# Query and key projected feature-major, split in the read stage and reloaded as stacked operands

## What is computed

```python
x = res.reshape(b, l, H, C)                                  # H 512, C 4
y = jnp.einsum('blhc,hoc->bloh', x, W)                       # then normalised over h
q = jnp.einsum('bli,oi->blo', q, qkv_w[0]).reshape(b, l, NH, HD)   # NH 16, HD 32; k, v alike
q = rope(q, pos); k = rope(k, pos)     # x1*cos - x2*sin, x2*cos + x1*sin
scores = jnp.einsum('bqhd,bkhd->bhqk', q, k) / np.sqrt(HD)   # causal mask
p = jax.nn.softmax(scores, axis=-1)
o = jnp.einsum('bhqk,bkhd->bqhd', p, v)
```

## Time and profile before

| | us |
|---|---|
| median of 3 runs | 2198.38 |
| lowest and highest | 2197.77, 2211.18 |
| the profiled execution: span | 2198.0 |
| setup and read stage | 0 to 342.4 |
| attention | 342.4 to 846.4 |
| block stage | 846.4 to 2198.0 |

### The profile page before, as it was taken

The page is one execution under the profiler, slowest core; times in us unless marked ns, Lnnn a source line. Parts: engine busy times, 40 slices in busy tenths (PEclk is TensorE's granted clock), DMA queues, the critical chain, the costliest instruction groups (busy, mean ns, idle before and its releaser), DMA issues.

```text
span 2198.0 us, 25095 instructions
## 1 busy us (share of the span) xinstructions
PE 1985.1 (90%) x9562; PEld 1379.5 (63%) x9562; DVE 1415.1 (64%) x1563; ACT 978.9 (45%) x1376; POOL 421.8 (19%) x325
## 2 busy tenths in 40 slices
PE   4789997999999995289989999999999999989998
PEld 0345556565656653157767777777777677766786
DVE  5587766677777756958657738658639558468100
ACT  4756652788787765054145323153341162432100
POOL 0000006576666540000000001010001000011111
PEclk8999996899999996599999999999999999999999
DMA  6547536686666743346666757776658777569675
GB/s 244 157 111 190 121 82 221 224 303 232 235 238 228 265 148 129 118 154 236 226 239 225 259 193 215 235 254 252 226 189 236 205 263 279 223 169 258 155 177 142
DMA packets 178876, 453.87 MB, mean 206 GB/s; under 512 B 64320, under 2 KB 64576, under 8 KB 161344
## 3 DMA queue, kind: packets, MB, share of 16 engines
q1 hardware_dynamic: 146160, 313.31, 42.4%
q0 software_dynamic: 30432, 128.46, 18.9%
q10 hardware_dynamic: 2160, 10.43, 1.3%
HBM read 304.80 MB, written 147.32 MB: 206 GB/s over the span
## 4 chain that ended last, share of the span: by engine, by line
PE 44%; DVE 7%; DMA 5%; ACT 4%; issue 2%; SPq 0%; POOL 0%; DVEq 0%; POOLq 0%; ACTq 0%
PE ps L1793 16%; PE ps L1603 8%; PE ps L1605 7%; PE ps L1604 7%; DMA sign_h<-sign_h_scratch 2%; DMA up<-up_s_scratch 2%; PE ps L1662 1%; PE ps L1671 1%; PE ps L1623 1%; ACT L1822 1%; DVE Y L2116 1%; PE ps L1712 1%; PE ps L1700 1%; DVE DL_attn L2023 0%; DVE E_attn L2028 0%
## 5 line engine op out<-in xcount | busy, mean ns | idle before, releaser
L1793 PE MATMUL ps<-XH,sign_h 128*128 128x512 f32 x768 | 307.1, 400 | 12.0 <-DMA sign_h<-sign_h_scratch 7.5
L1793 PE MATMUL ps<-XL,sign_h 128*128 128x512 f32 x768 | 300.8, 392 | 0.0
L1164 DVE TENSOR_REDUCE maxes<-ps 128x1 f32<-128x512 f32 (+3 forms) x384 | 207.8, 554 | 103.0 <-PE ps L977 78.7
L1603 PE MATMUL ps<-ZH,up 128*128 128x512 f32 x512 | 204.4, 399 | 13.4 <-DVE ZL L2141 8.9
L1605 PE MATMUL ps<-ZH,up 128*128 128x512 f32 x512 | 200.4, 391 | 0.0
L1604 PE MATMUL ps<-ZL,up 128*128 128x512 f32 x512 | 200.4, 391 | 0.0
L1091 ACT ACTIVATE probs<-ps 128x512 f32<-128x512 f32 (+3 forms) x384 | 167.5, 485 | 54.6 <-PE ps L1004 32.3
L1793 PEld LDWEIGHTS ps<-XH,sign_h 128*128 128x128 f32 x768 | 145.0, 189 | 59.3 <-issue 12.9
L974 PE MATMUL ps<-turned_k,turned_q 96*128 96x512 f32 (+3 forms) x384 | 159.5, 429 | 11.9 <-DVE maxes L1164 10.4
L1020 PE MATMUL ps<-probs,v_ones 128*64 128x512 f32 (+3 forms) x768 | 169.6, 520 | 0.3 <-ACT probs L1091 0.3
L1793 PEld LDWEIGHTS ps<-XL,sign_h 128*128 128x128 f32 x768 | 145.1, 189 | 31.2 <-issue 1.9
(11 more groups left out here) (334 smaller groups left out, 4173.8 us busy)
## 6 DMA issues: line engine op xcount, KB each, us to landing
sign_h<-sign_h_scratch SPq DMA_DIRECT2D x256, 256.0 KB, 4.0
up<-up_s_scratch SPq DMA_DIRECT2D x58, 1024.0 KB, 6.5
proj<-proj_s_scratch SPq DMA_DIRECT2D x58, 640.0 KB, 4.1
X<-in_x_read POOLq DMA_DIRECT2D x16, 1024.0 KB, 8.3
xn_scratch<-X SPq DMA_DIRECT2D x16, 1024.0 KB, 14.1
sign_raw<-in_sign SPq DMA_DIRECT2D x32, 512.0 KB, 8.0
sign_h_scratch<-sign_high SPq DMA_DIRECT2D x32, 512.0 KB, 4.1
sign_l_scratch<-sign_low SPq DMA_DIRECT2D x32, 512.0 KB, 5.2
```

Source lines behind the costliest of these rows:

```text
L1164: eng.tensor_reduce(MAXES[:, e, q, k0 // T:k0 // T + 1], ps[:, MX[m % 2], 0:w], AX.X, ALU.max).then_inc(mx_read.sem, mx_read.unit)
L1603: eng.matmul(out_ap, lh, rh, start=start, stop=False, skip_group_check=True)
L1793: mm = eng.matmul(ps[:, sign_bank(m)], s[q][:, f], x[:, n], start=n + w == 0, stop=n == NF - 1 and w == len(operands) - 1, skip_group_chec ...
```

## The change

- Setup computes the angles with 16 frequencies x 8 groups of tokens on the partitions, and SyncE writes the cosines and sines to a scratch in DRAM, from where each block's are loaded (`load_turns`).
- q and k are projected feature-major: weights are the stationary operand, 512 tokens the moving one; rows of the weights are reordered (`halves`) so that the first and the second rotary half of eight heads come out in two consecutive units of [128, 512]. `rope` takes two units, with six operations of VectorE. GpSimd splits each unit into a high and a low part (`cut`), and SyncE stores both. v stays as it was. Units live in four slots (`UNITS`) of two tiles; `free_unit` waits for the stores of the unit four before.
- Squares of x and y share two tiles in one order (`SQUARED`, `square_free`); some squares, centrings and variance products change places.
- In attention, twelve DMAs per pair (`operands`) load [high, high, low] and [high, low, high] straight into the operand tiles of three pairs in turn, those of pair 0 at the end of the read stage. `turn`, `take_high`, `take_low`, `out` and `take_v` are gone; v is used as loaded, from three tiles.
- The freed banks make three for maxima and row products together (`RING`, `ring_bank`, `ring_free`) and three for scores (`score_bank`).
- `weigh` has four products of 32 columns (v of head 0, ones, v of head 1, ones) instead of two of 64; `recip` and `head_out` take both heads at once.
- Low signs are no longer stored; the block stage would make them again on GpSimd if they were needed.

```diff
+def operands(tiles, qk_s, n):
+
+    b, e = n // (NH // 2), n % (NH // 2) * 2
+    i, row = e // (NH // 2), e % (NH // 2) * (HD // 2)
+    for o in range(2):
+        for j, k in enumerate(PARTS[o]):
+            for half in range(2):
+                at = j * HD + half * (HD // 2)
+                yield (tiles[o][at:at + HD // 2],
+                       qk_s[o, k, b, i, half, row:row + HD].rearrange("(e r) t -> r e t", e=2))
...
+        SQUARED = [("x", 0, g) for g in range(HC)] + [("y", 0, 0), ("y", 0, 1), ("x", 1, 0), ("x", 1, 1), ("y", 0, 2), ("x", 1, 2), ("x", 1, 3)]
+        for n in range(1, NB + 1):
+            order = [("y", n - 1, 2)] * (n > 1) + [("y", n, 0), ("x", n + 1, 0), ("x", n + 1, 1), ("y", n, 1), ("x", n + 1, 2), ("x", n + 1, 3)]
+            SQUARED += [x for x in order if x[1] < NB]
...
+        def square_free(eng, k):
+
+            if k >= 2:
+                kind, n, m = SQUARED[k - 2]
+                if kind == "x":
+                    eng.wait_ge(xv.sem, xv.at(n, m + 1))
+                else:
+                    eng.wait_ge(yv.sem, yv.at(n, 2 * m + 1))
...
+        def free_unit(eng, g):
+
+            if g >= UNITS:
+                eng.wait_ge(stored[g % UNITS].sem, stored[g % UNITS].at(0, 2 * (g // UNITS)))
...
+                def cut(n):
+                    for k in range(2 * TT):
+                        a = unit_of(n, 1, k) % UNITS
+                        eng.wait_ge(roped.sem, roped.at(n, k + 1))
+                        eng.tensor_tensor(HIGH[a][:], FULL[a][:], t["one"][:].to_broadcast([P, T]), ALU.mult).then_inc(split.sem, split.unit)
+                        eng.wait_ge(split.sem, split.at(n, 2 * k + 1))
+                        eng.tensor_tensor(LOW[a][:], FULL[a][:], HIGH[a][:].bitcast(F32), ALU.subtract).then_inc(split.sem, split.unit)
...
+                def store_qk(n, s, u):
+                    b, h, a = n // (L // T), n % (L // T), unit_of(n, s, u) % UNITS
+                    for k, tile in enumerate((HIGH, LOW)):
+                        eng.wait_ge(split.sem, split.at(n, 2 * ((s - 1) * TT + u) + k + 1))
+                        eng.dma_start(io["qk_s"][OUTPUT[s], k, b, u // 2, u % 2, :, h * T:(h + 1) * T], tile[a][:].bitcast(F32)
+                                      ).then_inc(stored[a].sem, stored[a].unit)
...
+                def load_turns(n):
+                    if n:
+                        eng.wait_ge(roped.sem, roped.at(n - 1, 2 * TT))
                     else:
...
+                        eng.wait_ge(t["turn_out"].sem, t["turn_out"].at(0, GROUPS))
+                    for g in range(GROUPS):
+                        eng.dma_start(t["TURN"][g * (HD // 2):(g + 1) * (HD // 2)], io["turn_s"][:, :, n * T:(n + 1) * T]
+                                      ).then_inc(turns_in.sem, turns_in.unit)
...
                     if n == NB:
-                        eng.wait_ge(xv.sem, xv.at(NB - 1, HC + 1))
-                        for tt in range(TT):
-                            eng.wait_ge(stored[tt].sem, stored[tt].at(L // T - 1, 3))
-                        for o in range(3):
-                            eng.dma_start(t["G"][o][:], io["qkv_s"][:, o, 0:1]).then_inc(w_in.sem, w_in.unit)
+                        for a in range(UNITS):
+                            eng.wait_ge(stored[a].sem, stored[a].at(0, 2 * (unit_of(L // T, 0) // UNITS)))
+                        eng.wait_ge(xn_out[0].sem, xn_out[0].at(NB // 2 - 1, C))
+                        eng.wait_ge(rd.sem, rd.at(NB - 2, 3 * HC))
+                        for dst, src in operands([tile[:].bitcast(F32) for tile in t["FIRST_QK"]], io["qk_s"], 0):
+                            eng.dma_start(dst, src).then_inc(first_in.sem, first_in.unit)
...
-                                mm = eng.matmul(ps[:, bank], zz[place][:, ic, tt * P:(tt + 1) * P], t[ww][:, bass.ts(o * HC + ic, H)],
-                                                start=step == 0, stop=step == 3 * HC - 1)
+                                if s:
+                                    mm = eng.matmul(ps[:, bank], t[ww][:, (o * HC + ic) * H + tt * P:(o * HC + ic) * H + (tt + 1) * P], zz[place][:, ic],
+                                                    start=step == 0, stop=step == 3 * HC - 1)
+                                else:
+                                    mm = eng.matmul(ps[:, bank], zz[place][:, ic, tt * P:(tt + 1) * P], t[ww][:, bass.ts(o * HC + ic, H)],
+                                                    start=step == 0, stop=step == 3 * HC - 1)
...
                 x_var(1, 0)
                 x_var(1, 1)
                 project(0, 0, 2, TT)
+                y_var(0, 2)
                 x_var(1, 2)
                 x_var(1, 3)
-                y_var(0, 2)
                 x_var_close(1)
...
                 def x_square(n, g):
                     eng.wait_ge(xn.sem, xn.at(n, g + 1))
-                    if g >= 2:
-                        eng.wait_ge(xv.sem, xv.at(n, g - 1))
-                    eng.activation(SQX[g % 2][:], X[:, n % 2, 4 * g:4 * g + 4], ACT.Square).then_inc(x_act.sem, x_act.unit)
+                    square_free(eng, SQUARED.index(("x", n, g)))
...
-                    past(eng, yv, n, 2 * s - 1)
-                    if n + s == 0:
-                        eng.wait_ge(w_low.sem, w_low.at(0, 1))
-                    eng.activation(SQY[:], Y[:, OUTPUT[s]], ACT.Square).then_inc(y_act.sem, y_act.unit)
+                    square_free(eng, SQUARED.index(("y", n, s)))
...
                         y_square(n, 0)
...
                         x_square(n + 1, 0)
-                        x_square(n + 1, 1)
...
                     if now:
                         y_var_copy(n, 0)
+                    if new:
+                        x_square(n + 1, 1)
+                    if now:
...
                         x_square(n + 1, 2)
-                        x_square(n + 1, 3)
...
                     if new:
+                        x_square(n + 1, 3)
...
+                def rope(n, s, i):
+                    k, g = (s - 1) * TT + 2 * i, unit_of(n, s, 2 * i)
+                    one, two = g % UNITS, (g + 1) % UNITS
+                    first, second = (ps[:, PJ[(n * 3 * TT + TT + k + j) % NP]] for j in range(2))
+                    cos, sin = t["TURN"][:, COS], t["TURN"][:, SIN]
+                    eng.wait_ge(pj.sem, pj.at(n, TT + k + 1))
+                    if s == 1 and i == 0:
+                        eng.wait_ge(turns_in.sem, turns_in.at(n, GROUPS))
+                    free_unit(eng, g)
+                    eng.tensor_tensor(FULL[one][:], first, cos, ALU.mult)
+                    free_unit(eng, g + 1)
+                    eng.tensor_tensor(OTHER[two][:], first, sin, ALU.mult).then_inc(pjq_used.sem, pjq_used.unit)
+                    eng.wait_ge(pj.sem, pj.at(n, TT + k + 2))
+                    eng.tensor_tensor(OTHER[one][:], second, sin, ALU.mult)
+                    eng.tensor_tensor(FULL[two][:], second, cos, ALU.mult).then_inc(pjq_used.sem, pjq_used.unit)
+                    eng.wait_ge(pjq_used.sem, pjq_used.at(n, k + 2))
+                    eng.tensor_tensor(FULL[one][:], FULL[one][:], OTHER[one][:], ALU.subtract).then_inc(roped.sem, roped.unit)
+                    eng.tensor_tensor(FULL[two][:], FULL[two][:], OTHER[two][:], ALU.add).then_inc(roped.sem, roped.unit)
...
                     scale(n - 1, 2)
                     if new:
                         x_centre(n + 1, 0)
+                        x_centre(n + 1, 1)
                     rope(n - 1, 1, 0)
-                    if new:
-                        x_centre(n + 1, 1)
-                    rope(n - 1, 1, 1)
                     if new:
                         x_centre(n + 1, 2)
                     z_low(n - 1, 2)
                     if new:
                         x_centre(n + 1, 3)
-                    rope(n - 1, 1, 2)
-                    rope(n - 1, 1, 3)
+                    rope(n - 1, 1, 1)
                     if now:
                         centre(n, 1)
                         scale(n, 0)
-                    for tt in range(TT):
-                        rope(n - 1, 2, tt)
+                    rope(n - 1, 2, 0)
+                    rope(n - 1, 2, 1)
...
-        TURN, MX, SC, O = (0, 1), (2, 3), 4, (6, 7)
...
+        MX, SC, O = (0, 1, 2), (3, 4, 5), (6, 7)
...
-        TURN_AT = {7: (0, 1), 8: (2, 3), 9: (4, 5), 11: (6, 7)}
...
+        RING, m = [], 0
+        for p in range(NSC):
+            RING += [("max", m + j) for j in range(sum(MAX_AT[p]))]
+            m += sum(MAX_AT[p])
+            if p in ROW_AT:
+                RING += [("row", ROW_AT[p], half) for half in range(2)]
+        NR = len(MX)
+
+        def ring_bank(n, x):
+
+            return MX[(n * len(RING) + RING.index(x)) % NR]
+
+        def ring_free(eng, n, x):
+
+            k = n * len(RING) + RING.index(x) - NR
+            if k >= 0:
+                n, y = k // len(RING), RING[k % len(RING)]
+                if y[0] == "max":
```

(48 more changed lines are left out.)

409 lines of the change are left out of this document (170 added, 239 removed).

## The result

| | before | after |
|---|---|---|
| median of the runs, us | 2201.01 (5 runs, 2197.77 to 2211.18) | 2187.38 (5 runs, 2180.57 to 2189.62) |
| profiled execution, span | 2198.0 | 2185.6 |
| setup and read stage | 342.4 | 367.0 |
| attention, to the first product of the block stage | 504.2 | 447.4 |
| block stage, from that product to the end | 1351.4 | 1371.2 |

The ratio after to before is 0.9929 (95% interval 0.9906 to 0.9953); a second set of runs gave 0.9920 (0.9898 to 0.9942). The change is faster by 0.7%, where 2.2% were forecast, and 2187 lies just above the range of 2113 to 2186. Attention gave 57 us, the read stage took 25 and the block stage, which the forecast left alone, took another 20.

A forecast was written before the change was run, and what follows sets the result against it. Attention was taken as bound by TensorE, the read stage by a ring of TensorE, VectorE and ScalarE dependences. Attention -74.8 and read stage +26.9 on 2198.0, plus 0.4 to the median, gave 2150 us, range 2113 to 2186.

The forecast's parts named there:

- That one is as before for this input: Block stage: stays at 1351.6 us because its low sign path is not taken; no change forecast.
- first joint period: Attention, after the front of pair 0: 37.0 us falls to 32.9, -4.1 us (bounds 0 and -9).
- Rival 3: Attention: SyncE's queue, 22 issues a pair, becomes the bound with a 33.3 us round; whole 2285 us; chance 0.08.
- The third maxima bank should [recover] 1.8: Steady attention: a third bank removes five waits of 0.35 us before maxima, 1.8 us a period.
- Steady periods: Attention: fourteen periods go from 28.4 to 24.3 us each, -55.2 us in all (bounds -68 and -28).
- Weighing in 32-column products: Attention: four 32-column products cost no more than two of 64; zero taken, bound +13 us.
- rival 2: Attention weighing: narrow 32-column products cost up to 0.9 us a period; whole 2164 us; chance 0.08.
- The front of pair 0: Start of attention: stacked operands are ready, so 30.4 us becomes 16.8, -13.6 us (bounds -16 and -6).
- The shared squares: Read stage: squares of x and y sharing two tiles delay ScalarE's work, +3.4 us (bounds 0 and 7).
- the order: Read stage, blocks 1 and 2: moved centring, square and its products cost +5.0 us each, +10 (bounds 2 and 12).
- the lock: Read stage, blocks 0 to 2: GpSimd cuts slow VectorE through the shared SBUF interface, +4.5 us (bounds 0 and 30).
- Rival 1: Read stage: VectorE operations wait for whole GpSimd cuts, 40 us instead of 4.5; whole 2186 us; chance 0.14.

The follow-up runs named there:

- turn_last: Changed kernel with only the scratch of the turns declared behind all others: 2177.47 us, ratio 0.9887 to the kernel before, block stage 1359.0 us.
- dram_as_before: Changed kernel with its DRAM scratches declared in the kernel before's order and sizes, new ones behind: 2173.28 us, block stage 1357.7 us.
- two_banks: Changed kernel with two banks instead of three in the ring of maxima and row products: steady period 26.02 us instead of 25.09.
- centre_back: Changed kernel with the second centring of x behind the first rope again: 2174.91 us, last projection ends at 348.8 us instead of 356.2.
- fill_cut: Changed kernel with each cut of q and k replaced by two zero fills: last projection 356.2 us, first maximum 361.82 instead of 367.0.

## Why the prediction was wrong

The failed steps are these.

- **"That one is as before for this input"** (the block stage), +19.8 us. Its program is the same, but the change alters the list of DRAM scratches, and placement alone lengthens the stage (1369.4 in the kernel before when shifted, 1359.0 in the changed one when put nearly back). I had read the diff for instructions and not for what it allocates. By whole times the placement is worth some 9 us (turn_last) to 15 (dram_as_before against the two kernels beside it), so it is not all of the 19.8 of that one profile.
- **No term for the first rounds of attention**, +10.9. I counted the twelve operand loads as 9.5 us ahead of ones rows and V, and not as ahead of the loads on which GpSimd's whole chain of splits hangs; its lateness reached TensorE two pairs later, by two ways. Part of these 10.9 us is the other side of the -6.5 in the first joint period. Rival 3 had the right mechanism (SyncE's queue and what stands on it) at the wrong place and price: in the steady periods the queue holds nothing.
- **"The third maxima bank should [recover] 1.8"**, mis-sized: 0.93 by two_banks, and 1.05 for all that is not transposes by the direct comparison. I took the 2 us between maxima and scores for waits; TensorE's idle time ahead of maxima was only 0.74 a period, and most of the difference (1.5 us) is still there without it. Steady periods gave -44.1 for -55.2.

Right by the runs: transposes out at 2.2 us a period. Start-to-start sums (ten periods before, eleven after) split the 3.3 us of 28.37 - 25.09 into 2.23 of transposes, 0.21 of maxima (8.34 to 8.13) and 0.82 of weighing (10.22 to 9.40); the last holds the wait of about 0.6 us that followed one weighing in each period. Weighing in 32-column products costs nothing: a group at 512 columns starts 0.99 us before what follows it (571.26 to 572.25) against 1.01, and start-to-start medians at 384, 256 and 128 columns (0.78, 0.57, 0.36) are those of 64-column products within 0.02, where no wait follows; rival 2 would have had 0.9 us a period more. By the Trainium skill's page "TensorEngine Tiling (Array Packing)", section "Performance Considerations", and its 60 cycles a product, the estimate was 1.2 us a period more. The trace does not agree: the groups are no longer. The front of pair 0 and the end were met within 2 us; the first maximum came as the stage opened, at 367.00.

That the read stage's total (+26.9 against +24.6) was met is in part luck, as its parts were wrong. The shared squares cost 4.2 us in block 0 (123.68 to 127.84 at the first product of q), forecast 3.4. The next 12.1 us came by the run of projections that starts at 260.16 before and at 276.45 after, where 10 were forecast for the order and up to 4.5 for the lock; centre_back gives back 7.4 of it by one centring alone, where I had given each of two blocks 2.2. The waits were sized about right and the granted clock behind them was left out: 17 us at 0.50 between 125 and 352 us, 3.4 in the kernel before. The lock of 4.5 in blocks 0 to 2 is not to be seen (fill_cut). From the last run of projections (316.70 to 333.33) to the stage's end another 8.0 came (9 forecast), 5.2 of it by the cuts. Rival 1, the lock setting the stage with 40 us, is refuted by the same run.

Not settled: what in an address matters; why the block stage is still some 6 us longer than the kernel before's with the scratches nearly back (1357.7 to 1360.8 in four runs against 1351.4 and 1354.9), of which more stretches at the lower clock are a part (14 and 17 us in dram_as_before and turn_last, 7 and 10 in the two profiles of the kernel before); and the 2.6 us wait for a square in the rows above, which was not tried.
